# Cross-attention and quantised FFN, one core: second context and key chunk ahead of the query weight, value-product copies ahead of statistics and normalised tiles

## What is computed

```python
# x: (8, 512, 512), ctx: (8, 77, 384), 8 heads of 64
h = layernorm(x)
q, k, v = h @ Wq, ctx @ Wk, ctx @ Wv            # per head: 64 columns
out = softmax(q @ k.T / 8) @ v                   # over the 77 context rows
x = x + out @ Wo + bo
h = layernorm(x)
xq = act_quant(h, clip_x)                        # one scale for the whole tensor: its largest value
gate, up = xq @ wquant(w_gate).T, xq @ wquant(w_up).T    # 1408 columns, one scale per weight row
h = act_quant(silu(gate) * up, clip_down)        # again one scale for the whole tensor
x = x + h @ wquant(w_down).T
```

## Time and profile before

| | us |
|---|---|
| runs of the kernel | 533.76, 534.18, 534.37 |
| profiled execution, its own time | 534.28 |
| its span | 532.5 |
| TensorE busy | 523.9 (98%) |
| VectorE busy | 448.7 (84%) |
| ACT busy | 288.9 (54%) |
| GpSimd busy | 229.4 (43%) |
| attention half, blocks 0 to 6 | up to about 253 |
| last tiles and scale | 253 to 297.5 |
| first FFN product | 297.5 to 452 |

### The profile page before, as it was taken

One profiled execution on the slowest core, in us unless ns is written; L12 is line 12 of the kernel. 1 busy time (PEld: TensorE's weight loads), 2 busy tenths in 40 slices (PEclk: granted clock), 3 DMA queues, 4 the chain that ended last, 5 costly groups with the idle time before them and its releaser, 6 DMA issues.

```text
span 532.5 us, 7840 instructions
## 1 busy us (share of the span) xinstructions
PE 523.9 (98%) x2659; PEld 352.8 (66%) x2666; DVE 448.7 (84%) x808; ACT 288.9 (54%) x416; POOL 229.4 (43%) x347
## 2 busy tenths in 40 slices
PE   8999999999999999999999999999999999999997
PEld 8888788787888888888777644444444445444444
DVE  4968798989989899898899689998999988776663
ACT  4844645565465654554435745545554543999300
POOL 4397679688596886866454000000000000055332
PEclk9999999999999999999999999999999999999999
DMA  8946365846667566435959984842243021499997
GB/s 307 315 180 183 112 180 187 285 155 211 221 196 245 182 224 190 153 111 169 224 84 353 247 207 180 319 120 44 77 118 94 26 41 30 163 334 209 135 111 127
DMA packets 82941, 93.81 MB, mean 176 GB/s; under 512 B 47085, under 2 KB 50157, under 8 KB 82645
## 3 DMA queue, kind: packets, MB, share of 16 engines
q1 hardware_dynamic: 77877, 84.13, 51.5%
q0 software_dynamic: 4320, 7.87, 9.9%
q10 hardware_dynamic: 704, 1.31, 0.8%
HBM read 47.51 MB, written 37.78 MB: 160 GB/s over the span
## 4 chain that ended last, share of the span: by engine, by line
PE 91%; DVE 4%; DMA 2%; issue 1%; SPq 1%; ACT 1%; POOL 0%; DVEq 0%
PE SP L653 14%; PE QO L648 14%; PE SP L450 6%; PE QO L415 4%; PE QO L414 4%; PE QO L413 4%; PE SP L693 4%; PE PTP L693 4%; PE QO L693 4%; PE PTP L483 3%; PE WOP L523 2%; PE WOP L525 2%; PE WOP L524 2%; PE MI L525 2%; PE MI L523 2%; PE MI L524 2%
## 5 line engine op out<-in xcount | busy, mean ns | idle before, releaser
L1599 POOL DMA_DIRECT2D out<-n2b x30 | 28.0, 974 | 204.6 <-DVE n2b L1410 204.5
L936 ACT ACTIVATE sil<-QO,fsc 128x512 f32<-128x512 f32 x87 | 59.8, 687 | 72.2 <-PE QO L648 71.3
L648 PE MATMUL QO<-nT,wgu 128*128 128x512 bf16 x340 | 87.2, 379 | 0.0
L653 PE MATMUL SP<-nT,wgu 128*128 128x512 bf16 x340 | 87.2, 379 | 0.0
L1357 DVE SCALAR_TENSOR_TENSOR h<-SP,fsc,sil 128x512 f32<-128x512 f32 x87 | 65.3, 750 | 16.1 <-PE SP L653 14.1
L1492 POOL TENSOR_TENSOR PN<-P,rs 128x512 f32<-128x512 f32 x64 | 44.6, 719 | 41.6 <-DVE rs L1019 41.6
L1363 DVE TENSOR_REDUCE hmx<-h 128x1 f32<-128x512 f32 x88 | 59.9, 685 | 2.9
L653 PEld LDWEIGHTS SP<-nT,wgu 128*128 128x128 bf16 x340 | 33.3, 98 | 40.1
L648 PEld LDWEIGHTS QO<-nT,wgu 128*128 128x128 bf16 x340 | 33.3, 98 | 40.1
L758 ACT ACTIVATE P<-P,r 128x616 f32<-128x616 f32 x32 | 25.9, 811 | 52.6 <-DVE P L1010 52.6
L965 ACT ACTIVATE h<-h,g 128x1536 int8<-128x1536 f32 (+2 forms) x38 | 44.3, 1262 | 0.0
(11 more groups left out here) (256 smaller groups left out, 1199.7 us busy)
## 6 DMA issues: line engine op xcount, KB each, us to landing
xTr<-in_xT SPq DMA_DIRECT2D x8, 1024.0 KB, 7.2
xn<-in_x SPq DMA_DIRECT2D x32, 256.0 KB, 4.0
out<-x SPq DMA_DIRECT2D x32, 256.0 KB, 3.1
n_rows<-n SPq DMA_DIRECT2D x32, 256.0 KB, 2.9
n2b<-n_rows SPq DMA_DIRECT2D x32, 256.0 KB, 3.6
out<-n2b POOLq DMA_DIRECT2D x30, 256.0 KB, 5.6
h_spill<-h SPq DMA_DIRECT2D x2, 2816.0 KB, 8.6
h<-h_spill SPq DMA_DIRECT2D x6, 768.0 KB, 8.0
```

The lines of the kernel that those rows point to most:

```text
L648: mm = e.matmul(QO[:, at:at + 512], wgu_v[:, k, cols(ic)], nT[:, b % 2, :, k, :], start=(k == 0), stop=(k == 3))
L653: mm = e.matmul(SP[:, at:at + 512], wgu_v[:, k, cols(NI + ic)], nT[:, b % 2, :, k, :], start=(k == 0), stop=(k == 3))
L936: e.activation(sil[:, n % SR, :], QO[:, (n % 2) * 512:(n % 2) * 512 + 512], ACT.Silu, scale=fsc[:, ic:ic + 1]).then_inc(silu, 1)
```

## The change

Four places of the programs are put in another order; one operation changes its engine.

1. **Start.** The second chunk of context and of key weight is issued ahead of the query weight, on SP's queue and on ACT's. TensorE does `k_chunk(1)` before the column sum; the eighth bank gets a function of its own behind the third chunk. VectorE splits chunk 1 before it adds up the weight and the context part of chunk 2 before it centres; the key low part of chunk 2 goes from VectorE to GpSimd. `q_first` waits for each operand by itself. ACT does the copies of the centred weight and of x in turns, with two bank copies in between.
2. **End of the set-up.** VectorE: statistics of tiles 5 and 6 earlier, the low part of value rows 4 (`v_low(4)`) behind `PV_low(0)`. ACT: rounding of weight tile 2 behind `PV_high(0)`. GpSimd: conversion of that tile behind four small vectors.
3. **Blocks 2 to 6.** ACT: `PV_high(b - 1)` ahead of `normed(s - 6)`.
4. **Last tiles.** ACT: `normed(22)` behind `PV_high(6)` and `PT_high(28)`. SP: `load_n2(0)` ahead of `store_n2(26)`.

The diff, cut to its core:

```diff
--- before.py
+++ after.py
...
@@ -370,18 +370,22 @@
                 w.wait_ge(ct_lo, k + 1)
                 for m in range(7):
                     k_part(m, k, 2)
-                if k == 2:
-                    w.wait_ge(wq_c, 4)
-                    for k0 in range(2):
-                        for i in (0, 2, 1):
-                            k_part(7, k0, i)
-                    k_part(7, 2, 0)
-                    k_part(7, 2, 2)
-                w.wait_ge(wk_lo, k + 1)
-                for m in range(8 if k == 2 else 7):
+                if k < 2:
+                    w.wait_ge(wk_lo, k + 1)
+                else:
+                    w.wait_ge(wk_lo_pool, 1)
+                for m in range(7):
                     mm = k_part(m, k, 1)
                     if k == 2:
                         mm.then_inc(k_mm, 1)
+
+            def k_last():
+
+                w.wait_ge(wq_c, 4)
+                for k in range(3):
+                    for i in (0, 2, 1):
+                        mm = k_part(7, k, i)
+                mm.then_inc(k_mm, 1)
             def q_pairs(m):
                 return [(wqs[:, 0, k, cols(m)], wqs[:, 1, k, cols(m)], xTs[:, 0, k, :], xTs[:, 1, k, :]) for k in range(4)]
@@ -390,15 +394,18 @@
                 w.wait_ge(K_act, 2)
                 bank, pairs = qo_bank("q", 0, 0), q_pairs(0)
                 for k in range(4):
+                    w.wait_ge(wq_hi, k + 1)
+                    w.wait_ge(xT_hi, k + 1)
+                    e.matmul(bank, pairs[k][0], pairs[k][2], start=(k == 0), stop=False)
                     if k < 3:
+                        w.wait_ge(xT_lo_dve, k + 1)
+                        e.matmul(bank, pairs[k][0], pairs[k][3], start=False, stop=False)
                         w.wait_ge(wq_lo_pool, k + 1)
-                    else:
-                        w.wait_ge(wq_lo_dve, 1)
-                    w.wait_ge(xT_lo_dve, k + 1)
-                    e.matmul(bank, pairs[k][0], pairs[k][2], start=(k == 0), stop=False)
-                    e.matmul(bank, pairs[k][0], pairs[k][3], start=False, stop=False)
-                    mm = e.matmul(bank, pairs[k][1], pairs[k][2], start=False, stop=(k == 3))
-                mm.then_inc(q_mm, 1)
+                        e.matmul(bank, pairs[k][1], pairs[k][2], start=False, stop=False)
+                w.wait_ge(wq_lo_dve, 1)
+                e.matmul(bank, pairs[3][1], pairs[3][2], start=False, stop=False)
+                w.wait_ge(xT_lo_dve, 4)
+                e.matmul(bank, pairs[3][0], pairs[3][3], start=False, stop=True).then_inc(q_mm, 1)
             def q_chunk(b, m):
                 if (b, m) == (0, 1):
@@ -534,10 +541,11 @@
             for _ in range(12):
                 e.matmul(WOP[:, 0:128], ones[:, :], ones[:, :], start=True, stop=True)
             k_chunk(0)
+            k_chunk(1)
             w.wait_ge(ws_sum, 3)
             e.matmul(WOP[:, :], ones[:, :], wsum[0], start=True, stop=True).then_inc(wq_sum, 1)
-            k_chunk(1)
             k_chunk(2)
+            k_last()
             q_first()
             for m in range(1, 4):
                 q_chunk(0, m)
@@ -789,18 +797,18 @@
             e.dma_start(wkr[:, 0, :], wk_v[0]).then_inc(ld_k[0], 16)
+            e.dma_start(wkr[:, 1, :], wk_v[1]).then_inc(ld_k[1], 16)
             e.dma_start(wqr[:, 2:4, :], wq_v[:, 2:4, :]).then_inc(ld_wq, 16)
-            e.dma_start(wkr[:, 1, :], wk_v[1]).then_inc(ld_k[1], 16)
             e.dma_start(wkr[:, 2, :], wk_v[2]).then_inc(ld_k[2], 16)
             for k in range(3):
                 split_k(k)
             for k in range(4):
+                if k == 2:
+                    k_out(0, 0)
+                    k_out(0, 1)
                 w.wait_ge(wq_c, k + 1)
                 copy(wqs[:, 0, k, :], wqr[:, k, :]).then_inc(wq_hi, 1)
-            for k in range(4):
                 split_hi(0, k)
-            k_out(0, 0)
-            k_out(0, 1)
             for m in range(1, 8):
                 k_out(m, 0)
             for k in range(3):
@@ -842,12 +850,13 @@
             PT_high(3)
             soft_exp(4)
             v_high(4)
-            w_round(2)
             for b in range(1, 7):
                 s = 4 * b
+                PV_high(b - 1)
                 if b > 1:
                     normed(s - 6)
-                PV_high(b - 1)
+                else:
+                    w_round(2)
                 PT_high(s)
                 if b > 1:
                     w_round(s - 1)
@@ -877,9 +886,9 @@
                 if s + 2 < 26:
                     w_round(s + 2)
                 normed(s - 3)
-            normed(22)
             PV_high(6)
             PT_high(28)
+            normed(22)
             soft_exp(29)
             soft_exp(30)
             normed(23)
@@ -975,8 +984,9 @@
             def split_k(k):
                 w.wait_ge(ct_hi, k + 1)
                 less(cts[:, 1, k, :], ctr[:, k, :], cts[:, 0, k, :]).then_inc(ct_lo, 1)
-                w.wait_ge(wk_hi, k + 1)
-                less(wks[:, 1, k, :], wkr[:, k, :], wks[:, 0, k, :]).then_inc(wk_lo, 1)
+                if k < 2:
+                    w.wait_ge(wk_hi, k + 1)
+                    less(wks[:, 1, k, :], wkr[:, k, :], wks[:, 0, k, :]).then_inc(wk_lo, 1)
             def k_out(m):
                 half, j = m // 4, m % 4
...
@@ -1100,23 +1111,24 @@
             split_k(0)
+            split_k(1)
             w.wait_ge(ld_wq, 32)
             e.tensor_tensor(wsum[0], wqr[:, 0, :], wqr[:, 1, :], ALU.add).then_inc(ws_sum, 1)
             e.tensor_tensor(wsum[1], wqr[:, 2, :], wqr[:, 3, :], ALU.add).then_inc(ws_sum, 1)
             w.wait_ge(ws_sum, 2)
             e.tensor_tensor(wsum[0], wsum[0], wsum[1], ALU.add).then_inc(ws_sum, 1)
-            split_k(1)
+            split_k(2)
             for k in range(4):
                 w.wait_ge(wq_sum, 1)
                 e.scalar_tensor_tensor(out=wqr[:, k, :], in0=WOP[:, :], scalar=-1.0 / D, in1=wqr[:, k, :],
                                        op0=ALU.mult, op1=ALU.add).then_inc(wq_c, 1)
-            split_k(2)
             for k in range(3):
                 split_lo(0, k)
+            k_out(1)
             w.wait_ge(wq_hi, 4)
             less(wqs[:, 1, 3, :], wqr[:, 3, :], wqs[:, 0, 3, :]).then_inc(wq_lo_dve, 1)
             split_lo(0, 3)
-            for m in range(1, 8):
+            for m in range(2, 8):
                 k_out(m)
             for k in range(3):
                 w.wait_ge(wv_hi, k + 1)
@@ -1170,17 +1182,16 @@
             PT_low(2)
             soft_max(4)
             soft_sub(4)
+            first_stats(5)
+            first_aggr(5)
             PT_low(3)
             soft_sum(4)
             soft_rec(4)
-            v_low(4)
+            first_stats(6)
+            first_aggr(6)
             w_top(2)
             w_scale(2)
             w_inverse(2)
-            first_stats(5)
-            first_aggr(5)
-            first_stats(6)
-            first_aggr(6)
             for b in range(1, 7):
                 s = 4 * b
                 if b > 1:
@@ -1195,6 +1206,8 @@
                 PV_low(b - 1)
                 if b > 1:
                     largest(s - 7)
+                else:
+                    v_low(4)
                 soft_max(s + 1)
                 soft_sub(s + 1)
                 PT_low(s)
@@ -1521,6 +1534,8 @@
                             pattern=[[-1, 128]], channel_multiplier=1).then_inc(const, 1)
+            w.wait_ge(wk_hi, 3)
+            less(wks[:, 1, 2, :], wkr[:, 2, :], wks[:, 0, 2, :]).then_inc(wk_lo_pool, 1)
             for k in range(3):
                 w.wait_ge(wq_hi, k + 1)
                 less(wqs[:, 1, k, :], wqr[:, k, :], wqs[:, 0, k, :]).then_inc(wq_lo_pool, 1)
...
@@ -1552,11 +1568,11 @@
             split_lo(2)
             w_integer(1)
             soft_norm(4)
-            w_integer(2)
             for n in (5, 6):
                 first_scale(n)
             for n in (5, 6):
                 first_bias(n)
+            w_integer(2)
             for b in range(1, 7):
                 s = 4 * b
                 if b > 1:
@@ -1677,8 +1693,8 @@
             e.dma_start(ctr[:, 0, :], ctx_v[0]).then_inc(ld_k[0], 16)
+            e.dma_start(ctr[:, 1, :], ctx_v[1]).then_inc(ld_k[1], 16)
             e.dma_start(wqr[:, 0:2, :], wq_v[:, 0:2, :]).then_inc(ld_wq, 16)
-            e.dma_start(ctr[:, 1, :], ctx_v[1]).then_inc(ld_k[1], 16)
             e.dma_start(ctr[:, 2, :], ctx_v[2]).then_inc(ld_k[2], 16)
             load_xT(0)
             e.dma_start(wvr[:, :, :], Wv.rearrange("(k p) n -> p k n", p=128)).then_inc(ld_wv, 16)
@@ -1743,12 +1759,11 @@
             store_x1(26)
             store_x1(27)
             store_n2(25)
+            load_n2(0)
             store_n2(26)
             for n in range(28, NT):
                 store_n2(n - 1)
                 store_x1(n)
-                if n == 28:
-                    load_n2(0)
             store_n2(31)
             load_n2(1)
```

(5 more changed lines are left out.)

## The result

The changed kernel took 538.21 us in the median of four runs (537.83 to 539.71); the kernel before took 534.17. The forecast was 534.8, at most 537.0: too low by 3.4. The profiled execution is the longest of the four, 539.71 with a span of 537.9, so its trace shows 5.4 us of loss where the median has 4.0.

What follows compares the result with a forecast made beforehand. It took TensorE, busy 152.00 of 152.00 us between 101 and 253 us, to bound the kernel. The terms -0.45 - 0.9 + 1.4 + 0.65 + 0.8 - 0.95 = +0.55 gave 534.8 us, range 532.3 to 537.0.

Steps and rivals of the forecast that it cites:

- The start, -0.45: At the start: second chunk ahead of the query weight brings the first query group's end and what follows 0.45 us earlier.
- its last product at 21.5 and the next group at 21.7: At the start: the first query group's last product at 21.5 us, the second group at 21.7, 0.5 earlier.
- Tile 5, -0.9: End of the set-up: the score matmul of tile 5 loses its 0.89 us wait for VectorE, a 0.9 gain.
- Block 1, +1.4: Block 1: weight tile 5 lands late, at 83.35 us, so the transpose of tile 7 gives back all 1.35 gained.
- the 6.1 behind the landing: Block 1: TensorE may transpose the next tile only 6.1 us after VectorE's maximum on the landed weight.
- The first of the twelve at 69.6: SyncE's queue, block 1: the first of twelve block-diagonal loads issued at 69.6 us, 1.95 later than before.
- tile 9 was given 0.65: Block 2: late load of x tile 11 and VectorE's dense run delay this score matmul by 0.65 us, between 0.3 and 1.0.
- Blocks 2 to 6, +0.8: Normalised tiles behind the copies make stores and twelve loads 2.65 us later; cost +0.8 in all for blocks 3 to 6.
- 2.9 costs nothing: Block 2: a weight load issued at 112.6 us and landing 2.9 later, at 115.5, does not delay TensorE's transpose.
- The tail, -0.95: Last tiles: 0.4 of the 0.85 us wait at tile 29 gets through, plus 0.55 at the matmul on the maximum.
- the queue is no limit: Last tiles: if x1 stores in the queue do not hold the residual back, the gain is 1.4 us, not 0.95.
- The rival: Blocks 1 to 5: late loads behind the twelve bound each block; 536.6, 536.7 or, with both, 538.5 us; chance 0.35.

Runs made afterwards that it cites:

- e10: Kernel before with only the start changed, but VectorE's copy of bank 1 behind its last low parts again: 533.48 us against 533.98 for the kernel before.
- e2: Kernel before with only the start changed, all of part 1: 534.03 us against 534.03 for the kernel before, ratio 1.0003.
- e5: Kernel before with only the end of the set-up changed, all of part 2: 536.64 us against 534.17 for the kernel before.
- e9: Changed kernel with 14 short matmuls on TensorE ahead of the transpose of tile 7: 537.46 us against 533.98 for the kernel before.
- e3: Kernel before with only ACT's order in blocks 2 to 6 changed, copies first: 536.72 us against 534.03 for the kernel before.
- e4: Kernel before with only the last tiles changed: 532.62 us against 534.03 for the kernel before, ratio 0.9976.
- e8: e5 with weight tile 3's store and weight tile 5's load ahead of the last eight of block 1's twelve loads: 534.10 us against 534.17 before.
- e12: e3 with the weight store and load ahead of the last eight of the twelve loads in blocks 2 to 6: 534.54 us against 533.98 before.
- e7: Kernel before with only VectorE's statistics of tiles 5 and 6 moved forward: 534.66 us against 534.17 for the kernel before.
- e1: Changed kernel with blocks 2 to 6 in ACT's old order: 534.93 us against 534.03 for the kernel before.
- e6: Kernel before with only VectorE's order at the end of the set-up changed: 537.33 us against 534.17 for the kernel before.

## Why the prediction was wrong, point by point

- **The start, -0.45.** Most of it came as forecast: column sum at 12.63 (near 12.6 was said) without idle before it, the first query group at 17.75 (17.9). The step that failed is "its last product at 21.5 and the next group at 21.7": they came at 22.27 and 22.61. The group took 4.86 us in place of 3.8. The third low part of x came 0.3 later than in the kernel before, although VectorE began its first three 1.0 earlier (they took 4.28 in place of 2.97; why was not tried), and TensorE waits 0.73 for it. The bank copy of 0.48 on VectorE ahead of the last two low parts was left out of the sum; e10 puts it at 0.4. Mis-sized by 0.9; at the end of the kernel e2 shows 0.0. The query weight, for which the forecast had 1.7 us of delay, was only 0.66 later (9.23), which helped nothing, as TensorE was at its second chunk until 12.63.
- **Tile 5, -0.9.** Right: 1.05 of gain, no wait.
- **Block 1, +1.4.** The mechanism was right, down to the 6.1 behind the landing (6.18 measured). Three sizes were wrong. "The first of the twelve at 69.6" came at 71.66: the low part ended 0.8 later than said, so that its store left at 68.63 (this is the start's 0.9 once more: in e5, without the start, the store leaves at 68.27, where the forecast would have it without the start's gain, 67.8 + 0.45), and the issues in between took 2.7 in place of 1.45, 0.75 of it a wait for GpSimd's conversion and 0.53 the longer issue of the wide weight load. So the weight landed at 84.9, not 83.35, and the transpose of tile 7 lost 1.75. Then the forecast let VectorE have its slack back: tile 9 was given 0.65, while it came a further 1.3 back. In the changed kernel TensorE's slow matmuls fill this time and no wait is left; e5, whose clock did not fall, shows what stands behind them: VectorE's dense run, late by the whole wait, puts tile 9 a further 1.0 back, with a wait of 1.16. e5 measured 2.6 for tile 9 and 2.5 for the kernel, where 1.4 + 0.65 less 0.9 stood in the sum.
- **The clock.** Not in the forecast. Between nothing (e5) and 0.7 us (e9).
- **Blocks 2 to 6, +0.8.** The forecast named the mechanism and the landing time (2.9) rightly and still took 1.9 too little: it asked only whether the transpose would wait ("2.9 costs nothing"), which indeed lost just 0.56 and 0.26 in blocks 2 and 3. What lost more in the four blocks together (2.1 against 1.1) was the score matmul of the next block's second tile, since each wait of VectorE for a weight (1.59, 1.30, 0.50, 2.27, 1.62) eats the slack that it had before the residual (10.3 us in six blocks before, 1.7 in two waits after). The part alone costs 2.7 (e3).
- **The tail, -0.95.** In the changed kernel it came as forecast, 0.9 by the trace, and for the reason given: the x1 slot held the residual back by 0.57, so that of the 0.85 only 0.45 got through (6.40 late at the transposes of tile 28, 5.95 at the residual). Alone it wins 1.4 (e4), the value that the forecast gave for "the queue is no limit", and there the slot held nothing back.
- **The rival.** "The loads behind the twelve become the bound of each block" is what happened; it had a chance of 0.35 and lay half outside the range. Its sign came too: VectorE waits over 1 us for a weight load in five blocks (2.50, 1.59, 1.30, 2.27, 1.62). That its 538.5 is near the measured 538.21 is partly luck: its price rested on landings of 5.1 us and on TensorE's transposes, and measured were landings of 2.9 to 3.1 and a loss that VectorE's missing slack carried to the score matmuls.

By parts the medians are 0.0 (start), +2.5 (set-up), +2.7 (blocks 2 to 6) and -1.4 (tail), in sum 3.8 against 4.0 measured. So close a match is partly chance: each part is known to 0.5 to 0.7 us by its interval, and the tail won 0.9 and not 1.4 in the changed kernel's trace.

The estimate for 256 KB that the forecast worked out from the fit in the Trainium skill ("DMA: Bandwidth & Descriptors", Anatomy of one DMA), 2.6 us, is near the 2.9 to 3.1 that the six weight loads behind the twelve took after the change; the 5.1 of the earlier trace rows did not come again in these, though other loads of this size in the same trace took up to 4.9. The price lay in the issue on SP, not in the transfer: ten microseconds for twelve small loads.

## What to carry to other kernels

In a queue that is strictly in order, ask of each step that is moved what stands behind it and who wants that first: twelve small loads of 0.7 to 0.9 us of issue each are a wall, and a tile needed soon belongs ahead of it (e8, e12). Price a wait on an engine with 92% load by its next two customers: the first may have slack, and the second pays. An instruction that frees up an engine wins nothing while its partner on the other engine waits for a third thing (e7).

## What the hardware showed that I had not expected

After 2.20 us of idle TensorE ran at half its clock for about 3.4 us, and in e1 after 2.12 us (granted clock 0.50 from 93 to 95 us). After 2.43 us of idle in the profiled run of e5 it did not fall, nor after 2.22 us in that of e6. The same kernel can do both: one of the four runs of the changed kernel had a mean clock of 1.00 where the other three had 0.997, and one of the five of e5 had 0.997. The same SP issue of the wide weight load took 0.43, 0.96 and 1.81 us, by where it stood; the cause was not tried.
